# Loading the other half of the sequence as bf16 into two buffers, and issuing its normalisation one block earlier

## The reference

```python
x = L0_attn_x                                   # (4, 4096, 1024)
xn = _layernorm(x, axis=-1)
q, k, v = split(xn @ w_qkv.T + b_qkv)           # 16 heads of 64
q = silu(q); k = softmax(k, over the sequence)
kv = einsum('bhnd,bhne->bhde', k, v)            # sums over all 4096 tokens
attn = layernorm(q @ kv) * sigmoid(gate(xn)) @ w_out.T + b_out
x = x + attn + moe(xn)
```

## Time and profile before

| | us |
|---|---|
| median of the two runs shown | 5831.26 |
| the two runs | 5421.77 and 6240.76 |
| profiled execution, its own time | 5418.04 |
| its span, slowest core (core 3) | 5416.5 |
| spans of all eight cores | 5404.1 to 5416.5 |
| TensorE busy, share of the span | 4775.9, 88% |
| VectorE busy | 822.4, 15% |
| ScalarE busy | 993.2, 18% |

### The profile page before, as it was taken

How to read it: one execution, slowest core, us unless ns; L and a number is a source line. 1 busy time by engine, 2 the same in 40 slices (tenths; PEclk the granted TensorE clock), 3 DMA queues, 4 the chain that set the end, 5 groups by cost and what they waited for, 6 DMA issues and landing times.

```text
span 5416.5 us, 51655 instructions; the slowest of 8 cores (5404.1 to 5416.5 us)
## 1 busy us (share of the span) xinstructions
PE 4775.9 (88%) x20848; PEld 2060.5 (38%) x20848; DVE 822.4 (15%) x1358; ACT 993.2 (18%) x1464; POOL 157.0 (3%) x318
## 2 busy tenths in 40 slices
PE   3665555576899999999999999999999999999997
PEld 0211111122344444444444444444444444444443
DVE  1223222435000010100101001011010110101101
ACT  0111111221302213022031220311202113021130
POOL 0000000000000000000000000000000000000000
PEclk8776667777999999999999999999999999999999
DMA  4000000100444444434444443444444444434444
GB/s 117 0 0 0 16 16 16 32 0 1 80 77 78 74 74 82 81 72 81 78 76 80 78 82 71 81 82 74 79 81 77 78 76 82 79 73 82 78 74 113
DMA packets 53195, 348.43 MB, mean 64 GB/s; under 512 B 6690, under 2 KB 7202, under 8 KB 13538
## 3 DMA queue, kind: packets, MB, share of 16 engines
q0 software_dynamic: 42416, 310.68, 31.6%
q1 hardware_dynamic: 10546, 34.45, 1.8%
HBM read 647.31 MB, written 8.45 MB: 121 GB/s over the span
## 4 chain that ended last, share of the span: by engine, by line
PE 86%; DVE 7%; issue 2%; ACT 2%; SPq 1%; DMA 1%; DVEq 0%; ACTq 0%; POOL 0%; POOLq 0%
PE pb L700 18%; PE pb L666 18%; PE pb L660 18%; PE pb L705 18%; PE pb L212 2%; PE pb L217 2%; PE pb L285 1%; PE pb L289 1%; PE pb L292 1%; PE pb L295 1%; DVE xsq L248 1%; DVE s_sb L349 1%; PE pb L566 1%; PE pb L338 1%; SPq L183 1%
## 5 line engine op out<-in xcount | busy, mean ns | idle before, releaser
L700 PE MATMUL pb<-h_sb,ring 128*128 128x512 bf16 x4608 | 1746.4, 379 | 31.7 <-ACT h_sb L676 31.7
L660 PE MATMUL pb<-xn,ring 128*128 128x512 bf16 x4608 | 1747.5, 379 | 0.7 <-ACT gfs L590 0.7
L666 PE MATMUL pb<-xn,ring 128*128 128x512 bf16 x4608 | 1747.6, 379 | 0.0
L705 PE MATMUL pb<-h_sb,ring 128*128 128x512 bf16 x4608 | 1746.6, 379 | 0.0
L672 ACT ACTIVATE h_sb<-pb,bfc_sb 128x512 bf16<-128x512 f32 x576 | 395.7, 687 | 3051.4 <-PE pb L666 3051.3
L700 PEld LDWEIGHTS pb<-h_sb,ring 128*128 128x128 bf16 x4608 | 450.8, 98 | 581.7 <-issue 40.1
L660 PEld LDWEIGHTS pb<-xn,ring 128*128 128x128 bf16 x4608 | 451.1, 98 | 545.3 <-issue 2.3
L666 PEld LDWEIGHTS pb<-xn,ring 128*128 128x128 bf16 x4608 | 451.0, 98 | 544.2 <-issue 1.1
L705 PEld LDWEIGHTS pb<-h_sb,ring 128*128 128x128 bf16 x4608 | 450.8, 98 | 541.6
L725 DVE SCALAR_TENSOR_TENSOR gatec<-pb,bpj_sb,gbc 128x512 f32<-128x512 f32 x128 | 96.1, 751 | 3157.1 <-PE pb L705 3157.1
L676 ACT ACTIVATE h_sb<-pb,bfc_sb 128x512 bf16<-128x512 f32 x576 | 395.7, 687 | 54.4 <-ACT h_sb L672 1.5
(11 more groups left out here) (106 smaller groups left out, 1609.7 us busy)
## 6 DMA issues: line engine op xcount, KB each, us to landing
ring<-wfc POOLq DMA_DIRECT2D x144, 1024.0 KB, 7.9
ring<-wpj POOLq DMA_DIRECT2D x144, 1024.0 KB, 7.9
acc<-x_own SPq DMA_DIRECT2D x8, 1024.0 KB
xo_sb<-x_oth SPq DMA_DIRECT2D x4, 2048.0 KB, 9.1
gbc<-gate_dram SPq DMA_DIRECT2D x16, 512.0 KB, 6.4
out<-acc SPq DMA_DIRECT2D x8, 1024.0 KB
wk_sb<-wk POOLq DMA_DIRECT2D x1, 2048.0 KB, 31.1
wv_sb<-wv POOLq DMA_DIRECT2D x1, 2048.0 KB, 46.2
```

The source lines that it names most:

```text
L660: op("tensor", lambda t, k=k, ml=ml, r=r, bka=bka, hf=hf: t.matmul(pb[bka][:], ring[r][:, k * 512 + ml * 128: k * 512 + ml * 128 + 128], x ...
L666: mm = op("tensor", lambda t, k=k, ml=ml, r=r, bkb=bkb, hf=hf: t.matmul(pb[bkb][:], ring[r][:, k * 512 + ml * 128: k * 512 + ml * 128 + 12 ...
L700: op("tensor", lambda t, m=m, r=r, bka=bka: t.matmul(pb[bka][:], ring[r][:, m * 128:(m + 1) * 128], h_sb[:, m * TH: m * TH + 512], start=( ...
L705: mm = op("tensor", lambda t, m=m, r=r, bkb=bkb: t.matmul(pb[bkb][:], ring[r][:, m * 128:(m + 1) * 128], h_sb[:, m * TH + 512: m * TH + 1024],
```

## The change

The loop over the other half's tiles is rewritten. `xo_sb` becomes two buffers in bf16, `xo_bf`, and `xno_sb` two buffers, `xno_b`; together they take the same room. The load moves from SyncE's queue to GpSimd's, which casts from f32 to bf16 on the way, and has a semaphore for each buffer. Tile 0 is loaded and normalised ahead of the loop. At the top of iteration s5 the load of tile s5 + 1 is issued; from the third load on it waits for the end of the normalisation that last read its buffer. The normalisation of tile s5 + 1 is issued between block 2 and block 3 of tile s5. In it the sum L212 is a matmul of bf16 by a bf16 column of ones (`onecb`, one more memset); the sum of squares L217 stays f32.

```diff
-    xo_sb = A("xo_sb", [128, NCH * 512], F32, AR + 32768)
-    xno_sb = A("xno_sb", [128, NCH * 512], BF16, AR + 49152)
+    xo_bf = [A(f"xo_bf{i}", [128, NCH * 512], BF16, AR + 32768 + i * 8192)
+             for i in range(2)]
+    xno_b = [A(f"xno{i}", [128, NCH * 512], BF16, AR + 49152 + i * 8192)
+             for i in range(2)]
...
+    onecb = A("onecb", [128, 1], BF16, SM + 16224)
...
-    SX = Sem("SX")
+    SX = [Sem("SX0"), Sem("SX1")]
...
+    op("gpsimd", lambda g: g.memset(onecb[:], 1.0), inc=(SGC, 1))
...
-    def emit_ln(src_fn, out_fn, bset, gamma_beta, ready, chunk_tgts=None):
+    def emit_ln(src_fn, out_fn, bset, gamma_beta, ready, chunk_tgts=None,
+                src_bf16=False):
...
-            mm1 = op("tensor", lambda t, c=c: t.matmul(
-                pb[b_s1][0:1, :], onec[:], src_fn(c),
+            mm1 = op("tensor", lambda t, c=c, src_bf16=src_bf16: t.matmul(
+                pb[b_s1][0:1, :], onecb[:] if src_bf16 else onec[:], src_fn(c),
...
+    def issue_xo_dma(s5):
+        par = s5 % 2
+        w = []
+        if st.get(("xo_free", par)) is not None:
+            w.append(st[("xo_free", par)])
+        op("gpsimd", lambda g, s5=s5, par=par: g.dma_start(
+            xo_bf[par].rearrange("p (c w) -> p c w", w=512),
+            d_xo.rearrange("(c p) t -> p c t", p=128)[:, :, s5 * 512:(s5 + 1) * 512]),
+            waits=w, inc=(SX[par], 16))
+        return (SX[par], SX[par].n)
+
+    def emit_oln(s5, dma_tgt):
+        par = s5 % 2
+        last = emit_ln(lambda c, par=par: xo_bf[par][:, c * 512:(c + 1) * 512],
+                       lambda c, par=par: xno_b[par][:, c * 512:(c + 1) * 512],
+                       (0, 1, 2, 3), None, [dma_tgt], src_bf16=True)
+        st[("xo_free", par)] = last
+        return last
+
+    xo_t = issue_xo_dma(0)
+    ln_o = [None] * 4
+    ln_o[0] = emit_oln(0, xo_t)
     for s5 in range(4):
-        dma_tgt = op("sync", lambda s, s5=s5: s.dma_start(
-            xo_sb.rearrange("p (c w) -> p c w", w=512),
-            d_xo.rearrange("(c p) t -> p c t", p=128)[:, :, s5 * 512:(s5 + 1) * 512]),
-            waits=[st.get("xo_free")] if st.get("xo_free") else [],
-            inc=(SX, 16))
-        ln_last = emit_ln(lambda c: xo_sb[:, c * 512:(c + 1) * 512],
-                          lambda c: xno_sb[:, c * 512:(c + 1) * 512],
-                          (0, 1, 2, 3), None, [(SX, dma_tgt)])
+        par = s5 % 2
+        if s5 < 3:
+            nxt_dma = issue_xo_dma(s5 + 1)
         for tb in range(4):
-            kv_block(lambda hc, tb=tb: xno_sb[:, hc * 512 + tb * 128:
-                                              hc * 512 + tb * 128 + 128],
-                     [ln_last])
-        st["xo_free"] = (SP, st["last_s"])
+            if tb == 3 and s5 < 3:
+                ln_o[s5 + 1] = emit_oln(s5 + 1, nxt_dma)
+            kv_block(lambda hc, tb=tb, par=par: xno_b[par][:, hc * 512 + tb * 128:
+                                                           hc * 512 + tb * 128 + 128],
+                     [ln_o[s5]])
```

## The result

The changed kernel takes 0.9941 of the time of the kernel before (95% interval 0.9927 to 0.9954): some 32 us less of 5420, no change by the 2% mark. Its profiled execution took 5388.39 us, with a span of 5386.9 on the slowest core, against 5418.04 and 5416.5; its other undisturbed executions took 5387.35 to 5395.64. (The median over all its executions, 5437.72, lies outside the forecast range of 5358 to 5407, which was drawn for an execution like the profiled one; it also counts executions in which a die ran for long at a lower granted clock, as 5831.26 did for the kernel before.)

A forecast was written before the change was run, and what follows sets the result against it. Expert matmuls were dearest but untouched; TensorE's waits for x_oth, reciprocal and VectorE's passes bounded the other half. Load ahead -26.9, sums -21.2, start +11.6 give -36.5 us: 5418.04 to 5381.5 us, range 5358 to 5407.

The forecast's parts named there:

- The start: Before the first normalisation: x_oth pieces on POOL's queue compete with SP's packets and delay it, +11.6 us (bounds 5.8 to 18.3).
- The step behind it: Loads at the start: the two queues alternate packet by packet, so 1800 x_oth pieces push in at 103 ns each.
- The other reading there: Loads at the start, by the skill's whole-packet rule: all 2048 x_oth pieces pass first, 13.2 us.
- The move: Normalisation issued ahead of a tile's block 3: the stall changes place and keeps its size, 0 us.
- The load ahead: Other half, tiles 1 to 3: loading x_oth one tile ahead removes three waits of the statistics, -26.9 us.
- The sums: Other half's statistics, four tiles: bf16 L212 shortens a chunk to 1.07 us, -21.2 us (bounds 0 and -27.5).
- Dear pieces: Loads at the start: cast pieces are paid by the piece, at 1309 ns a delay of 168 us, 5538; chance 0.04.
- An untouched start: First normalisation: the x_oth loads don't delay it, so -48.1 us alone, 5370; chance 0.13.
- Statistics that get no shorter: Other half's statistics: ScalarE sets the pace or the one-row matmul costs what it did, 5403; chance 0.10.
- Statistics that start at the upper clock: Statistics of three other-half tiles: 8.6 in place of 10.8 us each, 5375; chance 0.05.
- An other half at 0.81: Other half's tiles: three run at granted clock 0.81, costing 25 us, 5407; chance 0.05.
- A moved normalisation that hides: Normalisation ahead of block 3: it hides behind that block, three times 6.1 + 13.2 us more, 5324; chance 0.02.

## Why the prediction was right or wrong

**The start, right.** +11.6 us was forecast for the price of the two loads, the least disturbed cores show +11.5, and holding the loads back takes it away. That it is right to a tenth is in part luck: 2016 pieces passed where 1800 were counted, and each cost the start 91 ns and not 103. The step behind it was half right: pieces and packets do take turns about one for one when whole (1995 to 1771), but the run with half pieces shows that one for one isn't the rule. The other reading there, by which all of POOL's pieces pass first, is out as well: of 4096 half pieces 2574 to 3287 had passed.

**The move, right.** The two waits kept their size, and undoing the move changed nothing.

**The load ahead, mis-sized.** -26.9 us was forecast, -20.6 measured (429.7 to 409.1 on undisturbed cores). The wait itself was sized rightly: 27.0 us come back when the load isn't ahead. The step that failed was to count the idle time as the whole price and to carry the 4.5 us at the lower clock from a tile with a gap to tiles without one. There the lower clock holds longer: the short matmuls begin 5.9 us after the start, and it costs about 1 us in the statistics and 1 us in the block behind them, three times. The row that pointed to it, tile 0's 0.50, was read only as a sign that going without a gap is no better; next to a gap like these it is worse.

**The sums, right in the chunk, mis-sized in the clock.** -21.2 us forecast, about -25.7 measured where only they and the cast changed and the gap was still there: 21.1 of it in the four statistics, the rest in the blocks behind them, whose first 5 us in tiles 1 to 3 are granted 0.50 in the kernel before (core 7) and 0.64 to 0.68 here. The chunk of 1.07 us came out to the hundredth. But in the changed kernel, without the gap, the statistics take 11.3 to 11.5 us, where 10.8 was forecast for tiles 1 to 3; and tile 0 gave less than forecast, since it had taken 16.6 us on a core without core 3's 0.81, and not 18.4.

Both ways of counting meet. By the runs, -20.6 and -23.8 (the 25.7 less the 1.9 of longer waiting) make -44.4 us. Read straight from the least disturbed cores, core 7 before and core 5 after, the waits for x_oth that went were 25.1 us there and not core 3's 27.1, the statistics fall from 64.2 to 45.6 us, and some 1 us lies in the blocks: -44.3 in place of -48.1. On equal cores the sum is +11.5 - 44.3 and some -1 us elsewhere, -33.6 us (5404.1 to 5370.5), against -36.5.

**The slowest core.** The forecast was made on core 3, whose other half held a stretch at 0.81 (462.1 us in place of 453.5). After the change the slowest core 2 had none there, but one in the own half (432.7 us, where core 3 had 425.3), and 5.3 us more behind the last L343: +10.7 + 7.4 - 53.0 + 5.3 leaves -29.6 us of span. The sum had no term for such stretches; that they nearly cancel here, and that the profiled time comes within 7 us of the forecast, is in part luck.

**The rivals.** Dear pieces: falls, 91 ns of slip each where 376 were needed. An untouched start: falls. Statistics that get no shorter: falls, by the bf16 squares. Statistics that start at the upper clock: falls, with 0.50 in their first 5 us. The Trainium skill (TensorE: Matmul & The Clock Gate, section Why this matters for your kernels) has the clock fall back after an idle gap, and the statistics behind a gap do begin at the lower level here; but its advice to avoid the gap gave nothing, 0.50 without it against 0.67 with one of 9 us. An other half at 0.81: in stretches, on two cores of the profile, 5.3 us instead of the 25 at most. A moved normalisation that hides: falls for the change, and is true of the kernel that really takes it out of the queue.

## What to carry to other kernels

Issuing work earlier in program order hides nothing while its own matmuls stand in the same in-order queue ahead of the work that should cover it, or while it holds the banks that this work needs; split it, put the dependent matmuls behind the covering block, and free the banks by copies. A load that is taken off the critical path goes somewhere else: look at what it now queues beside, above all at the start, where one wait for a later semaphore gives the whole loss back. And when an idle gap of TensorE goes, price the work behind it at the clock that it gets without the gap.

## What the runs showed of the hardware

TensorE's granted clock over the first 5 us of the statistics was lower straight after its sparse 129-column matmuls than after a short stand-still: 0.50 against 0.67 after 9 us, in kernels that differ by the load ahead alone. It cost 6 of 27 us. It was not so behind every stand-still: 0.57 to 0.74 behind 44 of 50 gaps under 10 us, 0.50 to 0.55 behind 16 of 22 longer ones.

Two queues on the same DMA engines don't simply alternate by the trace's packets: 1.1 pieces of 1 KB (as written) to one packet of the other queue, but 1.46 to 1.87 pieces of half that size. By the slip of the start a whole piece cost 91 ns of one engine, a half piece 41.

Stretches at granted clock 0.81 come and go by execution, mostly by pairs of neighbouring cores: 10 to 12 us in the own half, 5 to 10 us in the other, in the kernel before too.
